# A finished image of a Winograd-style convolution: who adds the middle products, VectorE or a DMA

## The reference

```
xp  = log_pooling(x)                                  # 12 pooled maps per channel, fixed masks
out = conv(xp, w_conv1, stride (4, 3)) + conv(x, w_center) + b_center
out = (out - mean) * rsqrt(var + eps) * gamma + beta  # mean, var over images and pixels, per channel
return relu(out + x)
```

## Time and profile before

| | |
|---|---|
| median of 3 runs | 1685.85 us (1685.67 to 1686.25) |
| profiled execution | 1686.6 us, of which the span of the trace is 1684.8 us |
| TensorE busy | 1489.2 us, 88% |
| VectorE busy | 1531.3 us, 91% |
| ScalarE busy | 645.3 us, 38% |
| GpSimd busy | 2.7 us |
| one image in the steady part | 46.72 us |

### The profile page before, as it was taken

The page is one execution under the profiler, slowest core; times in us unless marked ns, Lnnn a source line. Parts: engine busy times, 40 slices in busy tenths (PEclk is TensorE's granted clock), DMA queues, the critical chain, the costliest instruction groups (busy, mean ns, idle before and its releaser), DMA issues.

```text
span 1684.8 us, 21919 instructions
## 1 busy us (share of the span) xinstructions
PE 1489.2 (88%) x8468; PEld 1476.5 (88%) x8468; DVE 1531.3 (91%) x1455; ACT 645.3 (38%) x689; POOL 2.7 (0%) x21
## 2 busy tenths in 40 slices
PE   6899999999999999999999999999999999993000
PEld 6899999999999999999999999999999999993000
DVE  8999999999999999999999999999999999995423
ACT  3234343343333434334333343433433334434423
POOL 0000000000000000000000000000000000000000
PEclk8999999999999999999999999999999999997555
DMA  2010111001111011100111101111011110149999
GB/s 110 20 38 29 38 38 38 21 27 38 38 38 38 29 38 38 38 29 19 38 38 38 38 29 38 38 38 37 11 38 38 38 38 29 38 159 421 425 424 382
DMA packets 28615, 129.54 MB, mean 77 GB/s; under 512 B 3520, under 2 KB 3520, under 8 KB 28608
## 3 DMA queue, kind: packets, MB, share of 16 engines
q1 hardware_dynamic: 23744, 103.77, 17.0%
q10 hardware_dynamic: 4864, 25.69, 3.7%
HBM read 78.88 MB, written 50.58 MB: 77 GB/s over the span
## 4 chain that ended last, share of the span: by engine, by line
PE 50%; DVE 27%; issue 11%; SPq 5%; ACT 4%; DMA 3%; DVEq 0%; ACTq 0%
PE acc L625 17%; PE acc L627 16%; PE acc L626 16%; DVE pooled_split L403 6%; DVE pooled L402 6%; DVE inner_split L403 5%; SPq L266 3%; ACT inner_split L324 3%; DVE box L402 2%; DVE y_stage L402 2%; DVE row L402 2%; DMA phase<-x 2%; SPq L263 2%; DMA out<-phase 1%; ACT phase L394 0%
## 5 line engine op out<-in xcount | busy, mean ns | idle before, releaser
L334 ACT ACTIVATE pooled_split<-pooled 128x1456 fp32r<-128x1456 f32 x192 | 273.4, 1425 | 608.0 <-DVE pooled L402 608.0
L403 DVE TENSOR_TENSOR pooled_split<-pooled,pooled_split 128x1456 fp32r<-128x1456 f32 x192 | 317.4, 1667 | 0.3 <-ACT pooled_split L334 0.3
L625 PE MATMUL acc<-inner_split,w_first 128*128 128x406 f32 (+1 forms) x640 | 225.7, 353 | 36.3 <-DVE y_stage L402 25.0
L625 PE MATMUL acc<-pooled_split,w_first 128*128 128x364 f32 x768 | 253.6, 330 | 2.4 <-DVE pooled_split L403 2.4
L625 PE MATMUL acc<-pooled_split,w_outer 128*128 128x364 f32 x768 | 252.3, 329 | 1.1 <-DVE pooled_split L403 1.1
L626 PE MATMUL acc<-pooled_split,w_first 128*128 128x364 f32 x768 | 252.6, 329 | 0.0
L627 PE MATMUL acc<-pooled_split,w_first 128*128 128x364 f32 x768 | 252.5, 329 | 0.0
L626 PE MATMUL acc<-pooled_split,w_outer 128*128 128x364 f32 x768 | 252.2, 328 | 0.0
L627 PE MATMUL acc<-pooled_split,w_outer 128*128 128x364 f32 x768 | 251.8, 328 | 0.0
L627 PE MATMUL acc<-inner_split,w_first 128*128 128x406 f32 (+1 forms) x640 | 222.8, 348 | 0.0
L625 PE MATMUL acc<-inner_split,w_inner 128*128 128x406 f32 (+1 forms) x640 | 221.2, 346 | 1.1 <-DVE inner_split L403 1.1
(11 more groups left out here) (82 smaller groups left out, 2200.7 us busy)
## 6 DMA issues: line engine op xcount, KB each, us to landing
x_pad<-x SPq DMA_DIRECT2D x64, 392.0 KB, 3.3
y_dram<-y_stage SPq DMA_DIRECT2D x31, 784.0 KB, 5.0
phase<-y_dram SPq DMA_DIRECT2D x30, 784.0 KB, 28.3
phase<-x SPq DMA_DIRECT2D x30, 784.0 KB, 30.5
out<-phase ACTq DMA_DIRECT2D x30, 784.0 KB, 16.0
w_stage<-w_raw SPq DMA_DIRECT2D x2, 896.0 KB, 7.7
out<-x_pad ACTq DMA_DIRECT2D x2, 784.0 KB, 20.4
w_stage<-w_raw SPq DMA_DIRECT2D x2, 768.0 KB, 9.1
```

Of the source, the lines that this page charges most:

```text
L334: nc.scalar.activation(view(pooled_split, 2 * j * PAIR, (1, PAIR)), view(pooled, (PAIRS * c + j) % 2 * PAIR, (1, PAIR)), ACT.Copy)\
L403: sub = lambda out_, a, b: nc.vector.tensor_tensor(out_, a, b, ALU.subtract)
L625: nc.tensor.matmul(place, hi_w, hi_in, start=start, stop=False)
```

## The change

The first output half and the second are no longer added on VectorE. `copy_y` on ScalarE copies banks 0 to 3 to `y_stage` (two instructions), ahead of `split_pooled` of pair 2 in the next image's step `c == 0`, and increments `y_copied`; TensorE's first inner product waits for that. The gathered middle products now lie in a buffer of their own, `middle_sums`, in the layout of `y_stage`. When an image has been copied and its middle products gathered, GpSimd issues one DMA that adds `middle_sums` to `y_stage` in SBUF (`accum_op`), and its completion is `y_ready`. SP's store, both calls of `measure` (now together in step `c == 1`, behind `split_inner`), and `make_pivot` wait for it. The last image keeps an addition on VectorE (`take_last_y`). `copy_m1` also waits for the previous image's transfer, and `copy_y` for the previous image's store and measures.

```diff
--- before.py
+++ after.py
@@ -98,7 +98,8 @@
         phase2 = sb("phase2", used[0])
         x_pad = sb("x_pad", CH * X_PAD)
         y_stage = sb("y_stage", CH * HW)
-        m1_copy = sb("m1_copy", CH * HALF)
+
+        middle_sums = sb("middle_sums", CH * HW)
 
         D1, D2, VD, SD = 0, MIDDLE, 2 * MIDDLE, 2 * MIDDLE + 2 * HALF
 
...
@@ -233,6 +237,17 @@
                 n += 1
             assert n == ZEROED
 
+            def add_middle(image):
+                pool.wait_ge(y_copied, CH * (image + 1) + FREE)
+                nc.gpsimd.sem_inc(y_turns, 1)
+                pool.wait_ge(middle_taken, image + 1 + FREE)
+                nc.gpsimd.sem_inc(y_turns, 1)
+                pool.dma_start(y_stage[:, :], middle_sums[:, :], accum_op=ALU.add).then_inc(y_ready, 16)
+
+            add_middle(0)
+            with pool.Fori(1, LAST) as image:
+                add_middle(image)
+
         @block.sync
         def _(sp):
             def load_x(image, c):
...
@@ -252,7 +267,7 @@
                         sp.wait_ge(x_used, CH * image + c + 1)
                         load_x(image + 1, c)
                 if not first:
-                    sp.wait_ge(y_ready, CH * image + FREE)
+                    sp.wait_ge(y_ready, 16 * image)
                     sp.dma_start(y_dram[bass.ds(image - 1, 1)].rearrange("n p f -> p (n f)"),
                                  y_stage[:, :]).then_inc(y_saved, 16)
 
...
@@ -337,17 +352,31 @@
 
             def copy_m1(image):
                 act.wait_ge(m_done, image + 1)
+                wait_from_one(act, y_ready, 16 * image)
                 wait_from_one(act, y_measured, MOMENTS * image)
-                nc.scalar.activation(view(m1_copy, 0, (HALF, CH), (H, U), (1, H)),
+                nc.scalar.activation(view(middle_sums, H, (HW, CH), (2 * H, U), (1, H)),
                                      view(acc, MBANK * BANK, (BANK, CH), (PITCH, U), (1, H)), ACT.Copy)\
                     .then_inc(m1_copied, 1)
 
+            def copy_y(image):
+
+                act.wait_ge(pooled_done, PAIRS * CH * (image + 1))
+                wait_from_one(act, y_saved, 16 * image)
+                wait_from_one(act, y_measured, MOMENTS * image)
+                for o in range(CH):
+                    nc.scalar.activation(view(y_stage, o * HW, (H, 2), (2 * H, U), (1, H)),
+                                         view(acc, 2 * o * BANK, (BANK, 2), (H, U), (1, H)), ACT.Copy)\
+                        .then_inc(y_copied, 1)
+
             def measure(image, o):
-                act.wait_ge(y_ready, CH * image + o + 1 + FREE)
+                if image is LAST:
+                    act.wait_ge(last_y_ready, o + 1)
+                else:
+                    act.wait_ge(y_ready, 16 * (image + 1))
                 act.wait_ge(pivot_ready, 1)
                 for kind, function in enumerate((ACT.Identity, ACT.Square)):
                     wait_from_one(act, y_measured, MOMENTS * image + KINDS * o + kind)
-                    nc.scalar.activation(m1_copy[:, :], view(y_stage, o * HW, (1, HW)), function,
+                    nc.scalar.activation(view(middle_sums, 0, (1, HW)), view(y_stage, o * HW, (1, HW)), function,
                                          bias=minus_pivot[:, o:o + 1],
                                          accum_out=sums[:, bass.ds((kind * CH + o) * IMAGES + image, 1)])\
                         .then_inc(y_measured, 1)
...
@@ -359,15 +388,16 @@
                         copy_m1(image - 1)
                     split_inner(s)
                     if c == 1 and not first:
-                        measure(image - 1, 1)
+                        for o in range(CH):
+                            measure(image - 1, o)
                     if first and c == 0:
                         split_weights(0, range(FIRST_OUTER_GROUP - 1, len(GROUPS)))
                         split_weights(1, range(len(GROUPS)))
                         act.wait_ge(warmed_up, 1)
                     for j in range(PAIRS):
+                        if c == 0 and j == 2 and not first:
+                            copy_y(image - 1)
                         split_pooled(s, c, j)
-                    if c == 0 and not first:
-                        measure(image - 1, 0)
 
             def tail_image(round_, d):
                 return LAST if round_ == d == 0 else SLOTS * round_ + d - 1
...
@@ -450,22 +480,23 @@
             def take_middle(image):
 
                 dve.wait_ge(m1_copied, image + 1)
-                wait_from_one(dve, y_saved, 16 * image)
-                wait_from_one(dve, y_measured, MOMENTS * image)
                 m2 = view(acc, (MBANK + CH) * BANK, (BANK, CH), (PITCH, U), (1, H))
-                m1 = view(m1_copy, 0, (HALF, CH), (H, U), (1, H))
-                add(view(y_stage, 0, (HW, CH), (2 * H, U), (1, H)), m2, m1)
-                sub(view(y_stage, H, (HW, CH), (2 * H, U), (1, H)), m1, m2).then_inc(middle_taken, 1)
-
-            def take_y(image):
-                dve.wait_ge(pooled_done, PAIRS * CH * (image + 1))
-                dve.wait_ge(middle_taken, image + 1 + FREE)
+                m1 = view(middle_sums, H, (HW, CH), (2 * H, U), (1, H))
+                add(view(middle_sums, 0, (HW, CH), (2 * H, U), (1, H)), m2, m1)
+                sub(m1, m1, m2).then_inc(middle_taken, 1)
+
+            def take_last_y():
+                dve.wait_ge(pooled_done, PAIRS * CH * IMAGES)
+                dve.wait_ge(middle_taken, IMAGES + FREE)
+                dve.wait_ge(y_saved, 16 * LAST)
+                dve.wait_ge(y_measured, MOMENTS * LAST)
                 for o in range(CH):
-                    y = view(y_stage, o * HW, (H, 2), (2 * H, U), (1, H))
-                    add(y, view(acc, 2 * o * BANK, (BANK, 2), (H, U), (1, H)), y).then_inc(y_ready, 1)
+                    columns = (H, 2), (2 * H, U), (1, H)
+                    add(view(y_stage, o * HW, *columns), view(acc, 2 * o * BANK, (BANK, 2), (H, U), (1, H)),
+                        view(middle_sums, o * HW, *columns)).then_inc(last_y_ready, 1)
 
             def make_pivot():
-                dve.wait_ge(y_ready, CH + FREE)
+                dve.wait_ge(y_ready, 16)
                 for o in range(CH):
                     for half in range(2):
                         link(nc.vector.bn_stats(pivot_stats[:, (2 * o + half) * 6:(2 * o + half + 1) * 6],
...
@@ -566,13 +597,11 @@
                     short_sum(s, c, 0)
                     short_sum(s, c, 1).then_inc(pooled_ready, 1)
                     lo_of_pooled(s, c, 1)
-                    if c == 0 and not first:
-                        take_y(image - 1)
                     lo_of_pooled(s, c, 2)
                     if second and c == 0:
                         make_pivot()
 
-            dve.sem_inc(y_ready, FREE)
+            dve.sem_inc(y_copied, FREE)
             dve.sem_inc(middle_taken, FREE)
             dve.wait_ge(zeroed, ZEROED)
             transform_weights(0)
...
@@ -581,7 +610,7 @@
             with dve.Fori(2, IMAGES) as image:
                 image_steps(image)
             take_middle(LAST)
-            take_y(LAST)
+            take_last_y()
 
             dve.wait_ge(y_measured, MOMENTS * IMAGES)
             link(nc.vector.reduce_sum(totals[:, :], view(sums, 0, (IMAGES, 2 * CH), (1, IMAGES)), AXIS_X))
...
@@ -654,7 +683,7 @@
                     pe.wait_ge(inner_lo_ready, 2 * s + 2)
                     for o in range(CH):
                         if c == 0:
-                            pe.wait_ge(y_ready, CH * image + FREE)
+                            pe.wait_ge(y_copied, CH * image + FREE)
                         for q, (with_v, with_d) in enumerate(((TAP_D, TAP_C), (TAP_A, TAP_F))):
                             place = view(acc, (2 * o + q) * BANK, (1, HALF))
                             at = VD + q * HALF
```

## The result

| | before | after |
|---|---|---|
| median | 1685.98 us (4 runs) | 1660.66 us (1659.88 to 1661.63, 4 runs) |
| ratio | | 0.985, 95% interval 0.9833 to 0.9867 |
| profiled execution, span | 1686.6, 1684.8 | 1659.88, 1658.1 |
| VectorE's last addition to `y_stage` starts | 1531.31 | 1504.64 |
| from there to the end of the span | 153.5 | 153.5 |

The gain is 25.3 us, forecast were 22.2. The two profiled spans differ by 26.7 us: the kernel before was profiled in an execution slower than its median, the kernel after in its fastest. Of the 26.7, 3.4 come before image 2's restart and 23.3 behind it, up to VectorE's last addition; the second phase is as long as before. A restart is TensorE's first inner product of an image, the one that waits for the banks.

A forecast was written before the change was run, and what follows sets the result against it. TensorE's wait for VectorE's take_y and the slow restart were taken to cost 0.79 us an image. 29 x 0.79 = 22.9 us, with +0.25 (start) and +0.5 (tail), gave -22.2 us: 1663.7 us, range 1656 to 1684.

The forecast's parts named there:

- TensorE needs 45.93 us alone: TensorE's time for one image without its wait for VectorE's take_y and the slow restart, against a period of 46.72 us.
- The worry that 0.25 us of it was the price of passing a wait: Rival, part of the stall stays: only 0.54 us per image is TensorE's wait proper; 15 us won, 1671 us, chance 0.07.
- The steady gain, 29 x 0.79 = 22.9 us: TensorE's stall of 0.79 us per image goes, over 29 periods from image 2's restart to image 31's.
- VectorE idles instead: Without take_y's 1.77 us, VectorE needs about 43.5 us per image and idles some 2 us before step c == 1's subtraction.
- The copies fit: ScalarE's two copies, 1.6 us, fit between the splits of pairs 1 and 2 with 0.3 us left; cover 3 us.
- A: Time from the end of copy_y to the landing of the adding transfer, taken as 9 us: 5.0 + 2 x 1.9.
- The estimate of 5.7 us from the Trainium skill: Alternative price of the adding transfer issued by GpSimd, 2.0 + 2 x 1.8 us, for a total some 3 us lower.
- The start: make_pivot waits once for the transfer; image 2 restarts at 137.05 for A = 9 against 136.81, costing 0.25 us.
- The tail: Second phase's first loads wait behind image 30's store; cost max(0, A - 8.5), 0.5 us for A = 9.
- Ring rival: Transfer, measures, split and VectorE's chain to the next copy_y take A + 31.7 us, slower if A exceeds 14.2; chance 0.11.
- Starved descriptors: Rival: GpSimd can't write descriptors beside busy VectorE, so A is about 15.5 us; +29 us, 1714 us, chance 0.07.
- the place of `take_y`: Position of take_y in VectorE's gapless chain, said alone to set TensorE's loss of 0.79 us per image.

The follow-up runs named there:

- take_y_early: The kernel before, with the unchanged take_y on VectorE one instruction earlier, ahead of lo_of_pooled(s, c, 1), no copy or transfer; 1661.70 us, ratio 0.9854.
- vector_adds: The changed kernel with the transfer replaced by one VectorE instruction adding middle_sums to y_stage, behind lo_of_pooled(s, c, 2); 1660.22 us, ratio 0.9846.
- detour_3: The changed kernel with three tiny transfers inside SBUF, one after the other, ahead of each adding transfer; 1671.84 us, ratio 0.9917.
- detour_2: The changed kernel with two tiny transfers inside SBUF, one after the other, ahead of each adding transfer; 1668.30 us, ratio 0.9896.
- plain_transfer: The changed kernel with a plain copy in place of the adding transfer, overwriting y_stage and leaving the sum out; 1657.81 us, ratio 0.9835.
- pe_waits_transfer: The changed kernel, but TensorE's first inner product waits for the transfer to land, not for ScalarE's copy; 1817.28 us, ratio 1.0777.
- detour_4: The changed kernel with four tiny transfers inside SBUF, one after the other, ahead of each adding transfer; 1732.62 us, ratio 1.0277.
- copy_late: The changed kernel with copy_y behind split_pooled of pair 2 instead of ahead of it; 1679.97 us, ratio 0.9963.
- detour_6: The changed kernel with six tiny transfers inside SBUF, one after the other, ahead of each adding transfer; 1869.44 us, ratio 1.1089.

## Why the prediction was right, step by step

- *TensorE needs 45.93 us alone.* The period is 45.93 in after, take_y_early, vector_adds and detour_3, and 45.92 in detour_2. The worry that 0.25 us of it was the price of passing a wait is gone: without a wait that holds, the price is nothing.
- *The steady gain, 29 x 0.79 = 22.9 us.* From image 2's restart to VectorE's last addition are 1371.2 us (133.44 to 1504.64), 23.3 fewer than the 1394.5 before.
- *VectorE idles instead.* Forecast 43.5 us of work and some 2 us of idle time, measured 43.52 and 2.00.
- *The copies fit.* Two took 1.52 us for the 1.6 forecast, with 3.2 us of cover for 3.
- *A = 9 us was mis-sized.* The forecast put it at 5.0 + 2 x 1.9, two extra passes over a plain store. The add costs what one extra pass does (plain_transfer), without the add it is 4.5 us from the copies' end to the landing, in place of the 5.0, and A is 6.6 us. The pessimistic term cost the forecast most of its 3.1 us of error: 2.4 at the start and 0.5 in the tail. With A = 6.6 its own sum gives 22.9 + 2.4 - 0.25 = 25.05 us, for 25.3 measured. The estimate of 5.7 us from the Trainium skill is close to the 5.8 us from the issue to the landing; it has no term for the 0.75 us from the copies' end to the issue, and so was 0.9 below A.
- *The start.* The forecast was a restart of image 2 at 128.05 + A, which gives 134.7 for A = 6.6, against a measured 133.44. VectorE's first instruction starts at 6.26 in this execution and at 7.16 before, which is 0.9 us; the two copies took 0.13 us less than forecast at each of images 0 and 1, and 0.1 us is left over. The 0.9 is no gain of the change: take_y_early, whose start is that of the kernel before, begins at 6.3 too.
- *The tail.* Forecast max(0, A - 8.5), so nothing at 6.6; measured 153.5 us for 153.5. At A = 11.1 it gives 2.6 and detour_2's second phase is 2.3 longer; at 13.3 it gives 4.8 and detour_3's is 4.4 longer.
- *Ring rival.* Its mechanism is real, its threshold 14.5 us, and A is less than half of that. *Starved descriptors:* ruled out, the issue came 0.75 us after the copies, 6.5 us before VectorE's first idle time (550.93). By the Trainium skill (SBUF — State Buffer, "Who interferes with whom") an addition of two tensors doesn't hold up descriptor writing; the trace agrees, with 0.86 us for an issue beside VectorE's row at 544.03.
- *What the prediction argued loosely.* It named the place of `take_y` as the cause, and yet entered VectorE's relief beside it, as if both were needed. take_y_early shows that the place alone was.

So the forecast's mechanism held, and its largest error was a term that was too large, 2.4 us too long for A. Two expectations missed: the period of pe_waits_transfer (the granted clock) and the time of detour_4 (A). That the last us of vector_adds got lost in the second phase was not pursued.

## What to carry to other kernels

When two engines are nearly full and wait for each other in turn, first look where in the late engine's queue the releasing instruction stands. Moving it ahead of one that nobody is waiting for gave the whole steady gain here, and offloading it to two other engines gave no more. Before hanging waits on a transfer, add up the ring it closes: here 6.7 us more of latency cost 11 us in all (detour_3), and the next 2.9 us cost 61 (detour_4). And leave room below the threshold: latency isn't fixed, and in detour_4 the same transfer took 0.8 us longer.

## What the runs showed of the hardware

- A transfer that adds inside SBUF took 2.05 times the engine time of a plain one of the same bytes (7.6% against 3.7% of the span) and landed 5.8 us after the issue against 3.6.
- GpSimd's issue of the adding transfer took 0.86 us (0.53 for a plain one) and was not held up by a VectorE that was busy without a gap with additions and subtractions.
- A wait of 3.4 us of TensorE was followed by 3.3 us at half pace and a granted clock of 0.50 (550.06 to 553.33), which added 1.6 us to the wait. Waits of 0.4 us (copy_late) and 1.5 us (detour_4) were followed by no such stretch: the second product came 0.28 or 0.29 us after the first, and then the pace was the full one, 0.18. In between both were seen: after a wait of 2.59 us (detour_6, 563.95) the pace stayed full, after one of 2.93 (detour_2, 138.15) it was full for two steps and then halved.
- With a load of x issued meanwhile, the adding transfer landed 6.6 us after its issue instead of 5.8 (detour_4), and GpSimd waited 2.2 to 3.3 us for a tiny one instead of 1.7 (detour_6).
